# A decoder kernel with a mixture of experts: the experts' rows are gathered by a list of places instead of being scattered into an inbox, and GpSimd makes every second lower comparison of the experts' weights

## The chip, the cores and the metric

One NeuronCore of one Trainium2 chip runs the whole program in one launch. The metric is the device time of one execution in microseconds (us). The engines are named as in the profile: PE (TensorE matmuls), PEld (its weight loads), DVE (VectorE), ACT (ScalarE), POOL (GpSimd) and SP (SyncE, which here only issues DMAs). L12 is line 12 of the kernel before.

## The reference

Six residual layers over x of shape (8, 512, 256), that is 4096 rows of 256 columns: self-attention, cross-attention with quantised weights, a grouped pair of matmuls, a mixture of experts, masked cross-attention, and a quantised pair. The change touches the mixture of experts and the end of the layer ahead of it. Cut to that layer:

```python
def act_quant(x):
    scale = 127.0 / max(max(abs(x)), 1e-5)          # by row
    return clip(round(x * scale), -128, 127) / scale
def weight_quant(w):
    scale = 1.0 / max(mean(abs(w)), 1e-5)           # one number for a matrix
    return clip(round(w * scale), -1, 1) / scale    # -1, 0 or 1
T, E, K, C = 4096, 8, 2, 512                        # C rows of room for each expert
xf = layernorm(x).reshape(T, 256)
probs = softmax(bitlinear(rmsnorm(xf), gate_in_norm_w, gate_w))
topw, topi = top_k(probs, K)
for each expert e:
    pos = cumsum(expert_mask[:, e] > 0) - 1         # place of a row in the expert's room
    tok = the rows with pos < C, in order; empty places give a row of zeros
    h = bitlinear(xf[tok], gp_norm_w[e], gp_w[e])   # gp_w[e]: 1024 x 256
    g, y = split(h)
    out = bitlinear(silu(g) * y, dp_norm_w[e], dp_w[e])   # dp_w[e]: 256 x 512
outputs[tok] += out * topw                          # a row gets what its two experts made
```

Rounding a weight matrix to -1, 0, 1 needs the mean of its magnitudes first (its limits are plus and minus half that mean), and then `(w > half) - (w < -half)`.

## The kernel before

The rows lie in SBUF as `X`, 32 tiles of 128 rows; tile `n` holds rows `128 n` to `128 n + 127`, and a sequence `b` (of B = 8) is four tiles. Each stage is a `Block`: every engine has a program of its own in it, the order of which is written out by hand, semaphores join them, and all engines meet at a barrier between two blocks. The three blocks that matter run one after the other.

**The middle block** (function `middle`) does cross-attention, the grouped pair and the gate. Its loop runs `b` over 12 steps, each sequence in it at several depths at a time. The PSUM banks are handed out in the order of the list `in_order`, round robin over eight; PE takes a bank with `take(bank)` when its last reader has given it free. `gate.u` holds the normalised rows that the experts will get; ACT writes them with `experts_rows(b)`, four instructions for a sequence. The routing is worked out in two parts, sequences 0 to 2 (12 tiles) in the middle block at step b = 7, and sequences 3 to 7 (20 tiles) at the start of the weights block. Each part is `gate.choose` on DVE (softmax, the two best experts; its last instruction gives `kept_made`), `gate.count` on PE (two matmuls that count the rows of each expert, bank "counts"), and `gate.slots` on DVE, which writes `m_slot`: for each row and each of its two experts the place, expert times 512 plus position. At step 7, PE runs `gate.count` ahead of `pair(7, 0)`, and DVE runs `gate.slots` last in the step, behind `add_outputs(6)`, `gate_roots(5)` and `gate_values(6)`.

**Sending.** `gate.send` on POOL scatters every tile of `gate.u` twice (once for each of the two experts of its rows) by an indirect DMA into the DRAM tensor `expert_in` (the inbox, 4096 rows), which SP has filled with zeros early in the middle block by eight DMAs from `f_outT`. 24 sends stand at the end of POOL's middle program, 40 in its weights program.

**The weights block** (first block of `experts`) rounds and transposes the weights of eight experts. Three buffers `g_stage` hold 3072 columns each (2048 of `gp_w`, 1024 of `dp_w`). For expert e: SP loads a buffer once `w_used` says it is free; ACT's `magnitudes(e)` sums the magnitudes; PE's `total(e)` adds them across partitions (one matmul); DVE makes the limits (L2270 to L2273), `g_below` (L2278, two instructions), and `g_w3` (L2284, two instructions, which wait for `w3_used`: PE must have turned the expert before); PE's `turn(e)` transposes `g_w3` in 24 matmuls (L2235, L2241); ACT's `turned_out(e)` copies them to `m_upT` and `m_downT` (L2210). The orders in the loops are

```python
# PE                                  # ACT
for e in range(E):                    for e in range(E):
    turn(e)                               turned_out(e)
    if e + BUFFERS < E:                   if e + BUFFERS < E:
        total(e + BUFFERS)                    magnitudes(e + BUFFERS)
```

SP ends this block by waiting for all 64 sends and loading the rows of experts 0 and 1 from the inbox.

**The experts block** (second block of `experts`) runs the experts one after the other. DVE's `rows(e)` (L2538) waits for `x_loaded`, SP loads expert e + 2 when expert e's rows are used. It lasts from 1504.6 to about 1650 us.

## Time and profile before

| | |
|---|---|
| runs shown (3) | median 2136.21 us, 2127.43 to 2140.68 |
| the profiled execution | 2119.09 us, span 2117.4 us from first to last instruction |
| busy, share of the span | PE 79%, DVE 71%, ACT 68%, POOL 38% |
| middle block | 1079 to 1411 us |
| weights block | 1411 to 1504.6 us |
| experts block | 1504.6 to about 1650 us |

The span is made of blocks between barriers, so the share of busy time says little about any one of them: PE is the busiest engine over the whole and nearly idle in the weights block. The view of the chain that ended last gives nothing here (it stops after one step, at the last line), so the chain within a block is read from the timelines: for each instruction they give its start, its duration, its engine, line, operand names and sizes, how many like it follow (x4), and in square brackets how long its engine stood idle before it and what ended that.

### The profile page before, as it was taken

How to read it: one execution, taken by the hardware profiler on the slowest of the kernel's cores; microseconds unless marked ns; L12 is line 12 of the kernel's file. 1: busy time of each engine (PE TensorE's matmuls, PEld its weight loads, DVE VectorE, ACT ScalarE, POOL GpSimd, SP SyncE). 2: the span in 40 equal slices, each digit the busy share in tenths (PEclk: the TensorE clock that was granted, in tenths of full speed). 3: DMA queues.
4: the chain of work that ended last, by engine and by line, in shares of the span. 5: the costliest groups of instructions: out<-in, count | busy, mean ns of one | idle time of the engine just before them, and what ended most of it. 6: DMA issues, size and time to landing. Idle time of an engine off the chain costs nothing. (4 is left out here: it accounts for less than half of the span.)

```text
span 2117.4 us, 42907 instructions
## 1 busy us (share of the span) xinstructions
PE 1667.2 (79%) x13316; PEld 1070.3 (51%) x13332; DVE 1493.2 (71%) x3066; ACT 1448.9 (68%) x2330; POOL 813.3 (38%) x893
## 2 busy tenths in 40 slices
PE   3889999999999999999758988513365588997677
PEld 1456565555555555555536766412233356665333
DVE  6877777777777877777561566657685487776765
ACT  2888988989898888989704567455387344444745
POOL 0434554545455554545500000048443456563000
PEclk9999999999999999999977989755567789998799
DMA  6222322223222232222151211045211411231002
GB/s 201 54 54 56 69 56 62 61 56 69 56 61 62 56 67 55 56 60 64 34 192 41 80 59 62 1 150 189 90 60 41 130 41 31 29 40 20 1 11 70
DMA packets 173821, 140.00 MB, mean 66 GB/s; under 512 B 83794, under 2 KB 155399, under 8 KB 173366
## 3 DMA queue, kind: packets, MB, share of 16 engines
q1 hardware_dynamic: 166710, 122.78, 21.7%
q0 software_dynamic: 6912, 14.71, 3.5%
q8 instruction: 108, 1.77, 0.4%
q14 instruction: 91, 0.75, 0.1%
HBM read 61.92 MB, written 20.97 MB: 39 GB/s over the span
## 5 line engine op out<-in xcount | busy, mean ns | idle before, releaser
L573 ACT ACTIVATE a_p_hi<-ps,a_probs_up,a_s_scale 128x512 f16<-128x512 f32 x512 | 398.1, 778 | 68.2 <-ACTq L571 66.9
L574 ACT ACTIVATE a_probs<-ps,a_probs_up,a_s_scale 128x512 f32<-128x512 f32 x512 | 398.2, 778 | 0.0
L688 DVE TENSOR_REDUCE a_top<-ps 128x2 f32<-128x1024 f32 x256 | 313.2, 1224 | 119.0 <-DVEq L687 119.0
L920 POOL TENSOR_TENSOR a_p_lo<-a_probs,a_p_hi 128x1024 f16<-128x1024 f32 x128 | 275.9, 2155 | 248.0 <-POOLq L919 205.0
L908 POOL TENSOR_TENSOR a_ops<-a_ident_down,a_top 64x256 f16<-64x256 f32 x256 | 159.8, 624 | 288.5 <-POOLq L903 280.0
L697 DVE TENSOR_TENSOR a_p_lo<-a_probs,a_p_hi 128x1024 f16<-128x1024 f32 x128 | 183.7, 1435 | 39.3 <-DVEq L696 39.3
L453 PE MATMUL ps<-a_v_hi,a_p_hi 128*128 128x65 f16 x2048 | 204.9, 196 | 4.4 <-PEq L448 4.2
L434 PE MATMUL ps<-a_ops 128*128 128x512 f16 x512 | 196.2, 383 | 15.0 <-PEq L432 14.5
L456 PE MATMUL ps<-a_v_lo,a_p_hi 128*128 128x64 f16 x2048 | 204.8, 195 | 0.0
L457 PE MATMUL ps<-a_v_hi,a_p_lo 128*128 128x65 f16 x2048 | 204.7, 196 | 0.0
L453 PEld LDWEIGHTS ps<-a_v_hi,a_p_hi 128*128 128x128 f16 x2048 | 190.9, 99 | 25.7 <-issue 14.9
L420 PE MATMUL ps<-a_qk,a_qd 128*128 128x512 f16 x512 | 152.7, 380 | 59.0 <-PEq L418 57.6
L435 PE MATMUL ps<-a_ops 128*128 128x512 f16 x512 | 196.7, 384 | 0.0
L456 PEld LDWEIGHTS ps<-a_v_lo,a_p_hi 128*128 128x128 f16 x2048 | 190.2, 100 | 12.1 <-issue 1.7
L457 PEld LDWEIGHTS ps<-a_v_hi,a_p_lo 128*128 128x128 f16 x2048 | 190.2, 99 | 0.0
L1189 POOL DMA_INDIRECT expert_in<-gate_u,m_slot x64 | 84.0, 1312 | 118.2 <-POOLq L1185 99.3
L407 PE MATMUL ps<-a_wp,a_oT 128*128 128x256 f32 x512 | 125.9, 390 | 1.1 <-PEq L363 1.1
L670 DVE SCALAR_TENSOR_TENSOR a_qk<-ps,a_qk 128x512 f16<-128x512 f32 x128 | 88.5, 692 | 35.7 <-DVEq L669 35.5
L420 PEld LDWEIGHTS ps<-a_qk,a_qd 128*128 128x128 f16 x512 | 44.3, 97 | 134.9 <-issue 107.1
L378 PE MATMUL ps<-a_xnT,a_wq 128*128 128x512 f16 x384 | 94.7, 383 | 6.3 <-PEq L363 6.2
L407 PEld LDWEIGHTS ps<-a_wp,a_oT 128*128 128x128 f32 x512 | 92.9, 191 | 11.4 <-issue 1.3
L378 PE MATMUL ps<-a_xnT,a_wk 128*128 128x512 f16 x384 | 94.6, 383 | 0.2
(499 smaller groups left out, 3709.4 us busy)
## 6 DMA issues: line engine op xcount, KB each, us to landing
a_ops<-a_qk SPq DMA_DIRECT2D x384, 128.0 KB, 2.3
...
a_qd<-a_qk SPq DMA_DIRECT2D x128, 64.0 KB, 2.2
...
```

The source lines that it names most:

```text
L378: last = nc.tensor.matmul(ps[:, JOB + bank, :], w[:, i, d, c * P:(c + 1) * P], xnT[:, j, d, :], start=(n == d == 0), stop=(n == len(PARTS) ...
L407: last = nc.tensor.matmul(ps[:, JOB + bank, 0:D], oT[:, c, t * P:(t + 1) * P], wp[:, c, :], start=(c % (HC // 2) == 0), stop=(c % (HC // 2 ...
L420: last = nc.tensor.matmul(ps[:, ROW + j % 2, :], qd[:, s, j, :], qk[:, s, K_HI, :], start=True, stop=True)
L434: nc.tensor.matmul(ps[:, st_bank(n), :], ops[:, s, i, A_K, keys], ops[:, s, i, A_Q, :], start=True, stop=False)
L435: nc.tensor.matmul(ps[:, st_bank(n), :], ops[:, s, i, B_K, keys], ops[:, s, i, B_Q, :], start=False, stop=True).then_inc(st_full, 1)
L453: first = nc.tensor.matmul(ps[:, AV, at:at + HD + 1], hi, v_hi[:, k, h, :], start=(k == 0), stop=False)
L456: nc.tensor.matmul(ps[:, AV, at:at + HD], hi, v_lo[:, k, h, :], start=False, stop=False)
L457: last = nc.tensor.matmul(ps[:, AV, at:at + HD + 1], lo, v_hi[:, k, h, :], start=False, stop=(k == KT - 1))
L573: nc.scalar.activation(p_hi[:, h % 2, k, :], scores, ACT.Exp, bias=probs_up[:], scale=s_scale[:])
L574: nc.scalar.activation(probs[:, h % 2, k, :], scores, ACT.Exp, bias=probs_up[:], scale=s_scale[:]).then_inc(st_taken, 1)
L688: nc.vector.tensor_reduce(top[:, c % 2, 2 * pair:2 * pair + 2], ps[:, ROW:ROW + 2, :], AX.X, ALU.max).then_inc(row_taken, 1)
L920: nc.gpsimd.tensor_tensor(p_lo[:, h % 2, 2:KT, :], probs[:, h % 2, 2:KT, :], p_hi[:, h % 2, 2:KT, :], ALU.subtract).then_inc(p_made_pool, 1)
```

## The change

The scatter and its inbox go. In the middle block SP stores the rows themselves, a sequence at a time, into a DRAM tensor `expert_rows` (eight DMAs of 512 KB behind the last weight loads, each waiting for its sequence's `u_made`); the eight DMAs of zeros are gone, and so are POOL's 24 sends there. `gate.slots` moves up on DVE to stand right behind `gate.choose`, `pair(7, 0)` moves ahead of `gate.count` on PE and in the list of banks, and on ACT `f_normalise(7)` moves ahead of `pair_turned(7, 0)` and `experts_rows(4)` from step 7 to step 8.

In the weights block the list of places is turned round: for each of the 4096 places, which row stands in it. DVE makes, for each of the 64 sets of 128 rows, a 0/1 matrix of the place's low part (`low`, 128 columns) and one of its high part (32 columns), the latter also times the tile's number and times the row's number (`numbered`, 64 columns); PE multiplies them, 64 matmuls into one bank; DVE reads the result behind expert 0 into `row_at`. POOL then gathers, four indirect DMAs for an expert, straight to where the experts block reads them (`x_in` is now `gate.u`). Between them POOL makes `below_odd`, the lower comparison of the next odd expert. DVE makes the limits of two experts at a time ahead of the even one, and `total` and `magnitudes` stand one expert later in their loops.

```diff
+            if b < B:
+                in_order += [("pair", b, 0)]
             if b - 1 in CHOICE:
                 in_order += [("counts", CHOICE.index(b - 1))]
-            if b < B:
-                in_order += [("pair", b, 0)]
...
+                for b in range(B):
+                    sp.wait_ge(u_made, b + 1)
+                    sp.dma_start(gate.rows[b * S:(b + 1) * S, :].rearrange("(t p) d -> p t d", p=P),
+                                 gate.u[:, b * TT:(b + 1) * TT, :]).then_inc(gate.stored, 16)
...
+                    if b < B:
+                        pair(b, 0)
                     if b - 1 in CHOICE:
...
                         gate.count(pe, part, bank_of["counts", part])
-                    if b < B:
-                        pair(b, 0)
...
+                    if b == B:
+                        experts_rows(B - 1 - QUANTISE)
...
+                    if b == B - 1:
+                        f_normalise(b)
...
-                    if 0 <= b - QUANTISE < B:
+                    if 0 <= b - QUANTISE < B and b != B - 1:
                         experts_rows(b - QUANTISE)
...
                     if b - 1 in CHOICE:
                         gate.choose(dve, CHOICE.index(b - 1))
+                        bank = bank_of["counts", CHOICE.index(b - 1)]
+                        gate.slots(dve, CHOICE.index(b - 1), bank, free[bank])
...
-                    if b - 1 in CHOICE:
-                        bank = bank_of["counts", CHOICE.index(b - 1)]
-                        gate.slots(dve, CHOICE.index(b - 1), bank, free[bank])
...
-                    sp.wait_ge(gate.sent, 16 * K * NT)
-                    for e in range(2):
-                        load(sp, e, e)
...
+                    pool.wait_ge(row_made, 1)
+                    pool.sem_inc(row_made, -1)
+                    for e in range(E):
+                        for t in range(RT):
+                            nc.gpsimd.indirect_dma_start(
+                                out=x_in[:, e, t, :], out_offset=None, in_=gate.rows,
+                                in_offset=bass.IndirectOffsetOnAxis(ap=row_at[:, e * RT + t:e * RT + t + 1], axis=0),
+                                bounds_check=NT * P - 1, oob_is_err=False).then_inc(x_loaded[e], 16)
+                        if e % 2 == 0:
+                            pool.wait_ge(limits_made, 1)
+                            pool.sem_inc(limits_made, -1)
+                            w = stage[(e + 1) % BUFFERS]
+                            for i, part in ((0, slice(0, W_UP)), (1, slice(W_UP, W_ALL))):
+                                nc.gpsimd.tensor_scalar(below_odd[:, part], w[:, part], minus_half_w[:, 1, i:i + 1], None, ALU.is_lt)
+                            pool.drain().then_inc(below_made, 1)
...
                         turned_out(e)
-                        if e + BUFFERS < E:
-                            magnitudes(e + BUFFERS)
+                        if 1 <= e and e - 1 + BUFFERS < E:
+                            magnitudes(e - 1 + BUFFERS)
...
+                    pe.wait_ge(places_made, 1)
+                    pe.sem_inc(places_made, -1)
+                    for n in range(N):
+                        last = nc.tensor.matmul(ps[:, PLACES, 0:2 * HIGH], low[:, n, :], numbered[:, n, :], start=(n == 0), stop=(n == N - 1))
+                    last.then_inc(places_full, 1)
                     for e in range(E):
                         turn(e)
-                        if e + BUFFERS < E:
-                            total(e + BUFFERS)
+                        if 1 <= e and e - 1 + BUFFERS < E:
+                            total(e - 1 + BUFFERS)
...
+                    nc.vector.tensor_tensor(high, of_places(number[:, 0:HIGH], HIGH), of_rows(high_no, HIGH), ALU.is_equal)
+                    dve.drain()
+                    nc.vector.tensor_tensor(low, of_places(number[:], P), of_rows(low_no, P), ALU.is_equal)
...
+                        nc.vector.tensor_tensor(numbered[:, i * NT:(i + 1) * NT, 0:HIGH], high[:, i * NT:(i + 1) * NT, :],
+                                                number[:, 0:NT].unsqueeze(2).broadcast_to([P, NT, HIGH]), ALU.mult)
+                    nc.vector.tensor_scalar(numbered[:, :, HIGH:2 * HIGH], high, number_p[:], None, ALU.mult)
+                    dve.drain().then_inc(places_made, 1)
...
+                    def rows_at_places():
+                        dve.wait_ge(places_full, 1)
+                        dve.sem_inc(places_full, -1)
+                        nc.vector.tensor_scalar(row_no[:], ps[:, PLACES, 0:HIGH], float(P), None, ALU.mult)
...
+                        nc.vector.tensor_scalar(row_at[:], row_no[:], 0.0, None, ALU.add)
+                        dve.drain().then_inc(row_made, 1)
+
+                    for e in range(E):
+                        j = e % BUFFERS
+                        if e % 2 == 0:
+                            limits(e)
+                            limits(e + 1)
+                            dve.drain().then_inc(limits_made, 1)
...
+                        below_e = below if e % 2 == 0 else below_odd
+                        if e % 2 == 0:
+                            for i, w, part in parts:
+                                nc.vector.tensor_scalar(below[:, part], flat(w), minus_half_w[:, 0, i:i + 1], None, ALU.is_lt)
+                            dve.drain()
+                        else:
+                            dve.wait_ge(below_made, 1)
+                            dve.sem_inc(below_made, -1)
                         if e:
                             dve.wait_ge(w3_used, 1)
                             dve.sem_inc(w3_used, -1)
...
                         dve.drain().then_inc(w_round, 1)
                         dve.drain().then_inc(w_used, 1)
+                        if e == 0:
+                            rows_at_places()
```

**PE, middle block, step 7.** Before: the two counting matmuls of the first part (96 columns) stand between the matmuls of `outputs(6)` (L1483) and those of `pair(7, 0)` (L1459). Names: `f_w2T` is the turned second weight, `outT` the transposed outputs, `c_free0` the bank that is taken.

```order
L1483 MATMUL ps<-f_xnT,f_wT 128x512
L1143 MATMUL ps<-gate_kept,gate_upto 128x96 [waits gate_kept_made,c_free0]
L1144 MATMUL ps<-gate_kept,gate_all 128x96
L1459 MATMUL ps<-f_w,f_w2T 128x257 [waits c_w2T_out,c_b1_set,c_free1]
L1459 MATMUL ps<-f_w,f_w2T 128x257 x7
L1496 MATMUL ps<-ident,f_outT 128x128 [waits c_outT_out,c_free2]
L1496 MATMUL ps<-ident,f_outT 128x128 x3
```

Now (the same rows of the changed program):

```order
L1472 MATMUL ps<-f_xnT,f_wT 128x512
L1448 MATMUL ps<-f_w,f_w2T 128x257 [waits c_w2T_out,c_b1_set,c_free0]
L1448 MATMUL ps<-f_w,f_w2T 128x257 x7
L1144 MATMUL ps<-gate_kept,gate_upto 128x96 [waits gate_kept_made,c_free1]
L1145 MATMUL ps<-gate_kept,gate_all 128x96
L1485 MATMUL ps<-ident,f_outT 128x128 [waits c_outT_out,c_free2]
L1485 MATMUL ps<-ident,f_outT 128x128 x3
```

The 8 matmuls of `pair(7, 0)` stand ahead of the wait for `gate_kept_made` now, and the counts use the bank behind the pair's.

**PE, weights block, from the first `turn` on.** `g_w_sum` is what `magnitudes` made (the matmul is `total`), `g_w` with `ident` are the transposes of `turn`. Before:

```order
L2225 MATMUL ps<-g_w_sum,g_ones 128x2 [waits g_w_part] x3
L2235 MATMUL ps<-ident,g_w 128x128 [waits g_w_round]
L2235 MATMUL ps<-ident,g_w 128x128 x15
L2241 MATMUL ps<-ident,g_w 128x128 x8
L2225 MATMUL ps<-g_w_sum,g_ones 128x2 [waits g_w_part]
L2235 MATMUL ps<-ident,g_w 128x128 [waits g_w_round,g_w_out]
L2235 MATMUL ps<-ident,g_w 128x128 x15
L2241 MATMUL ps<-ident,g_w 128x128 x8
L2225 MATMUL ps<-g_w_sum,g_ones 128x2 [waits g_w_part]
```

Now:

```order
L2244 MATMUL ps<-g_w_sum,g_ones 128x2 [waits g_w_part] x3
L2272 MATMUL ps<-gate_u 128x64 [waits g_places_made]
L2272 MATMUL ps<-gate_u 128x64 x63
L2254 MATMUL ps<-ident,g_w 128x128 [waits g_w_round]
L2254 MATMUL ps<-ident,g_w 128x128 x15
L2260 MATMUL ps<-ident,g_w 128x128 x8
L2254 MATMUL ps<-ident,g_w 128x128 [waits g_w_round,g_w_out]
L2254 MATMUL ps<-ident,g_w 128x128 x15
L2260 MATMUL ps<-ident,g_w 128x128 x8
L2244 MATMUL ps<-g_w_sum,g_ones 128x2 [waits g_w_part]
L2254 MATMUL ps<-ident,g_w 128x128 [waits g_w_round,g_w_out]
L2254 MATMUL ps<-ident,g_w 128x128 x15
```

The 64 matmuls on the matrices of places (they lie in `gate_u`) stand ahead of `turn(0)`; `turn(1)` follows `turn(0)` at once, and `total(3)` follows `turn(1)`.

**DVE, weights block, experts 2 and 3.** L2270 and L2315 read the sum of magnitudes. Before (expert 2, and the first row of 3):

```order
L2270 TENSOR_SCALAR m_w_mean<-ps 128x1 [waits g_w_total]
L2270 TENSOR_SCALAR m_w_mean<-ps 128x1
L2272 TENSOR_SCALAR g_half_w<-m_w_mean 128x2
L2273 TENSOR_SCALAR g_minus_half_w<-m_w_mean 128x2
L2278 TENSOR_SCALAR g_below<-g_stage,g_minus_half_w 128x2048
L2278 TENSOR_SCALAR g_below<-g_stage,g_minus_half_w 128x1024
L2284 SCALAR_TENSOR_TENSOR g_w<-g_stage,g_half_w,g_below 128x2048 [waits g_w3_used]
L2284 SCALAR_TENSOR_TENSOR g_w<-g_stage,g_half_w,g_below 128x1024
L2270 TENSOR_SCALAR m_w_mean<-ps 128x1 [waits g_w_total]
```

Now (from the last two rows of the limits of expert 2 to the rounding of expert 3):

```order
L2317 TENSOR_SCALAR g_half_w<-m_w_mean 128x2
L2318 TENSOR_SCALAR g_minus_half_w<-m_w_mean 128x2
L2315 TENSOR_SCALAR m_w_mean<-ps 128x1 [waits g_w_total]
L2315 TENSOR_SCALAR m_w_mean<-ps 128x1
L2317 TENSOR_SCALAR g_half_w<-m_w_mean 128x2
L2318 TENSOR_SCALAR g_minus_half_w<-m_w_mean 128x2
L2342 TENSOR_SCALAR g_below<-g_stage,g_minus_half_w 128x2048
L2342 TENSOR_SCALAR g_below<-g_stage,g_minus_half_w 128x1024
L2351 SCALAR_TENSOR_TENSOR g_w<-g_stage,g_half_w,g_below 128x2048 [waits g_w3_used]
L2351 SCALAR_TENSOR_TENSOR g_w<-g_stage,g_half_w,g_below 128x1024
L2351 SCALAR_TENSOR_TENSOR g_w<-g_stage,g_half_w,g_below_odd 128x2048 [waits g_below_made,g_w3_used]
L2351 SCALAR_TENSOR_TENSOR g_w<-g_stage,g_half_w,g_below_odd 128x1024
```

Each `g_w_total` is a wait for one more expert's sum. Two of them stand ahead of expert 2's comparison now; expert 3 has no comparison of its own on DVE but a wait for `g_below_made`, which POOL gives.

## Rows read from the trace of the kernel before

**Rows 1.** Busy time by stretch: us, then PE, PEld, DVE, ACT, POOL busy (instructions), clock, DMA share, GB/s.

```profile
1428.00:1495.00 67.00, 21.70 (x180) 19.98 (x180) 48.16 (x64) 37.71 (x45) 55.40 (x37) 0.53 0.45 150
```

**Rows 2.** Groups of DVE's instructions in the weights block, 1428 to 1495 us.

```profile
L2284 DVE SCALAR_TENSOR_TENSOR g_w<-g_stage,g_half_w,g_below 128x2048 bf16<-128x2048 f32 x8 | 18.8, 2351 | 14.8 <-DVEq L2282 9.8 <-PEq L2243 4.9
L2278 DVE TENSOR_SCALAR g_below<-g_stage,g_minus_half_w 128x2048 bf16<-128x2048 f32 x8 | 10.3, 1286 | 0.7
L2284 DVE SCALAR_TENSOR_TENSOR g_w<-g_stage,g_half_w,g_below 128x1024 bf16<-128x1024 f32 x8 | 10.2, 1279 | 0.0
L2278 DVE TENSOR_SCALAR g_below<-g_stage,g_minus_half_w 128x1024 bf16<-128x1024 f32 x8 | 6.0, 748 | 0.0
```

**Rows 3.** Timeline of DVE in the weights block: first limits, three of the eight roundings.

```profile
1428.31 0.22 DVE L2270 TENSOR_SCALAR m_w_mean<-ps 128x1 f32<-128x1 f32 x2 [0.63 <-DVEq L2267]
...
1431.00 3.55 DVE L2284 SCALAR_TENSOR_TENSOR g_w<-g_stage,g_half_w,g_below 128x2048 bf16<-128x2048 f32 x2
...
1437.70 3.55 DVE L2284 SCALAR_TENSOR_TENSOR g_w<-g_stage,g_half_w,g_below 128x2048 bf16<-128x2048 f32 x2 [0.18 <-DVEq L2282]
...
1491.35 3.55 DVE L2284 SCALAR_TENSOR_TENSOR g_w<-g_stage,g_half_w,g_below 128x2048 bf16<-128x2048 f32 x2 [0.36 <-DVEq L2282]
```

**Rows 4.** Timeline of ACT in the weights block: copies out and magnitudes.

```profile
1437.68 1.03 ACT L2210 ACTIVATE m_downT<-ps 128x1024 bf16<-128x1024 bf16 x1
...
1450.08 1.92 ACT L2201 ACTIVATE g_junk<-g_stage 128x2048 bf16<-128x2048 f32 x1
...
1453.12 0.19 ACT L2201 ACTIVATION_READ_ACCUMULATOR g_junk<-g_stage 128x1 f32 x1
...
1498.18 1.03 ACT L2210 ACTIVATE m_downT<-ps 128x1024 bf16<-128x1024 bf16 x1
```

**Rows 5.** Timeline of PE in the weights block: `total(4)` and the start of `turn(2)`.

```profile
1453.51 0.56 PE L2225 MATMUL ps<-g_w_sum,g_ones 128*128 128x2 f32 x2 [4.58 <-PEq L2224]
1453.93 1.87 PE L2235 MATMUL ps<-ident,g_w 128*128 128x128 bf16 x16
```

**Rows 6.** Timeline of POOL in the weights block: one send that waited, the last send.

```profile
1438.00 2.90 POOL L1189 DMA_INDIRECT expert_in<-gate_u,m_slot  x1 [0.30 <-issue]
...
1498.68 0.97 POOL L1189 DMA_INDIRECT expert_in<-gate_u,m_slot  x1 [0.31 <-issue]
```

**Rows 7.** The instructions on `e_r` on POOL: ns min/median/max.

```profile
L2358 POOL TENSOR_SCALAR e_r<-e_a,e_per_row x32: 478/479/1552, 1508.6 to 1601.7; 128x256 f16<-128x256 f32 x32
```

**Rows 8.** Two groups of POOL's instructions over the whole span.

```profile
L920 POOL TENSOR_TENSOR a_p_lo<-a_probs,a_p_hi 128x1024 f16<-128x1024 f32 x128 | 275.9, 2155 | 248.0 <-POOLq L919 205.0 <-POOLq L926 26.6 <-POOLq L885 11.6
...
L940 POOL TENSOR_SCALAR a_lny_tmp<-a_lny_tmp 128x4 f32<-128x4 f32 x21 | 4.6, 221 | 3.6 <-issue 3.6
```

**Rows 9.** Timeline of DVE and of POOL in the masked attention: the same operation beside POOL and alone.

```profile
1694.90 2.52 DVE L2107 SCALAR_TENSOR_TENSOR X<-b_got,m_share,X 128x256 f32<-128x256 f32 x2
1695.16 1.97 POOL L2712 TENSOR_TENSOR x_s<-x_s,x_top 128x1024 f32<-128x1024 f32 x1 [1.58 <-POOLq L2711]
...
1708.94 1.66 DVE L2107 SCALAR_TENSOR_TENSOR X<-b_got,m_share,X 128x256 f32<-128x256 f32 x4
```

**Rows 10.** Timeline of the end of the middle block, PE, DVE and ACT.

```profile
1347.24 0.24 PE L1143 MATMUL ps<-gate_kept,gate_upto 128*128 128x96 bf16 x1 [6.78 <-PEq L1379]
1354.34 1.29 DVE L1969 TENSOR_TENSOR X<-ps,X 128x512 f32<-128x512 f32 x2 [7.40 <-DVEq L1967]
1369.91 0.71 DVE L1155 TENSOR_TENSOR_SCAN gate_before<-gate_ones_col,ps 128x12 f32<-128x12 f32 x8
1374.93 0.17 DVE L1892 TENSOR_SCALAR gate_square<-mean_var 128x4 f32<-128x4 f32 x1 [0.17 <-issue]
1382.44 1.29 DVE L1969 TENSOR_TENSOR X<-ps,X 128x512 f32<-128x512 f32 x2 [0.49 <-DVEq L1967]
1405.22 2.07 ACT L1732 ACTIVATE gate_u<-X,gate_u_shift,gate_u_factor 128x256 f32<-128x256 f32 x4
```

**Rows 11.** Timeline of SP and DVE between the weights block and the experts block.

```profile
1500.77 0.92 SPq L2144 DMA_DIRECT2D e_x_in<-expert_in  x2
...
1504.79 1.23 DVE L2538 TENSOR_TENSOR e_a<-e_x_in,e_up_n 128x1024 f32<-128x1024 f32 x1
```

116 lines of the change are left out of this document (59 added, 57 removed).

## The prediction

> **What bounds the kernel now.** The blocks run one after the other, so I read the change's two blocks by their own timelines: first the busy times by stretch, then the groups of DVE, then the timelines of DVE, ACT, PE and POOL of the weights block, then the end of the middle block.
>
> In the weights block DVE is busy 48.2 of 67 us, POOL 55.4, ACT 37.7, PE 21.7 [rows 1]. No engine is full; a ring of waits sets the pace. DVE's first limits start at 1428.31 and its last rounding ends at 1491.35 + 3.55 = 1494.90 [rows 3]: 66.6 us for eight experts, 16.65 for a pair. The shortest step is seen between the first two roundings: the first ends at 1434.55, PE turns, the next starts at 1437.70, 3.15 later [rows 3]. So a rounding can end every 3.55 + 3.15 = 6.7 us. What the eight steps take beyond that is in the 14.8 us that DVE stood idle ahead of L2284 [rows 2]: PE holds `turn(1)` back behind `total(3)`, and so on. **The comparison L2278 (1286 + 748 ns [rows 2]) lies inside the 3.15 us in which PE turns**, so it costs next to nothing on the path. POOL's sends end at 1499.65 [rows 6], also after DVE; SP then loads rows at 1500.77 and the next block starts at 1504.79 [rows 11].
>
> **Places, first expert (added, on the path).** DVE must make the matrices of places ahead of its first limits. Two-input operations: 2351 ns for 2048 columns and 1279 for 1024 [rows 2], so 1.05 ns a column and 0.2 fixed. `high` has 2048 columns: 2.35; `low` 8192: 8.8; the tile's number, two of 1024: 2.55; the row's number, one input, 2048: 1.3 as L2278. The small casts and subtractions and their drains I take at 1.5, and the two added slot copies at 0.2. Sum 16.7 us; nothing covers it, since POOL and PE wait for it. The limits of experts 0 and 1 then start at 1445.0. The limits of one take 2.69 - 2.03 = 0.66 [rows 2, 3]; two, then the comparison, then the rounding: 1445.0 + 1.3 + 0.1 + 2.05 + 3.55 = 1452.0. Meanwhile PE makes 64 matmuls on two-byte numbers; 16 transposes take 1.87, 0.117 each [rows 5], so 7.5 us, to about 1452, hidden by the rounding. DVE reads the result (three small operations): 1453.2. POOL now issues four gathers ahead of its first comparison, although the limits have long been there: 0.97 + 0.30 each [rows 6], 5.5 us with the wake-up, to 1458.7.
>
> **POOL's comparison.** No row shows one. Nearest is a one-input `TENSOR_SCALAR` of 256 columns, 479 ns, beside 221 for 4 columns [rows 7, 8]: 1.02 ns a column. Two instructions, 3072 columns: 3.1 + 0.4 = 3.55 us. The upper end is the two-input rate, 2155 ns for 1024 columns [rows 8], 6.5 us. I take 3.55, as the form is the same. By the Trainium skill (GPSIMD Engine Reference, 3.1) a loop that makes a truth value takes 2.03 cycles an element unless it is unrolled, an estimate of 5.2 us, and the sum would be some 7 us worse. DVE waits for it: rounding 1 starts at 1458.7 + 3.55 + 0.3 and ends at **1466.3, against 1441.25 before**.
>
> **The pair's ring (added, on the path).** For experts 2 and 3 DVE makes both limits first, so expert 2 waits for `total(3)`, which stands behind `turn(1)`; and `magnitudes(3)` stands behind `turned_out(1)`. From the end R of an odd rounding: copies end at R + 4.15 (1434.55 to 1438.71 [rows 3, 4]); magnitudes 3.25 (1450.08 to 1453.31) and 0.2 until PE starts [rows 4, 5]; the sum 0.56 [rows 5]; limits 0.66 and drains 0.3: R + 9.1. Comparison 2.05, rounding 3.55, then 6.7 for the odd one, since PE must turn the even: R + 21.4. From the second pair on, PE does `total(4)` between `turn(2)` and `turn(3)`, which comes when `magnitudes(4)` ends, 1.2 us after the odd rounding: R + 22.6. Loads (issued when a rounding ends) land before ACT wants them; in each pair they have over 10 us.
>
> **The port between DVE and POOL.** Beside POOL's L2712 (1695.16 to 1697.13) two DVE operations take 2.52 us, where four take 1.66 [rows 9]: the second began when POOL ended. The other way, a send of 0.97 lasts 2.90 inside a rounding [rows 6]. So I add the whole 3.55 us to each of the three later pairs, in which POOL's comparison is due at the same time as DVE's. The Trainium skill (SBUF — State Buffer, Who interferes with whom) speaks against this change with the same rule: whichever of the two starts first has the shared port for its whole instruction and the other stands still; by it the trace agrees, and without it the sum is 10.6 us less. POOL's eight gathers between two comparisons take 10.2 us, some 14 with such stalls, and fit into the 26 of a pair.
>
> Last rounding: 1466.3 + (21.4 + 3.55) + 2 x (22.6 + 3.55) = 1543.5, against 1494.9: **+48.6 us**. At the end of the block the wait for the sends and SP's loads go: ACT ends 1499.21 - 1494.90 = 4.3 after the last rounding [rows 3, 4], plus 3.3 for the barrier (2.9 from the end of SP's issue at 1501.69 to the next block [rows 11], some 4 at the end of the middle [rows 10]), 7.6, against 9.7 before: -2.1. The experts block is unchanged: DVE found its rows at once before [rows 11], so loading them early buys nothing there.
>
> **The middle block (a gain).** PE stood idle 6.78 us ahead of the counts, DVE 7.40 us ahead of the add at 1354.34, and then DVE had `slots` (1369.91 to 1374.93, 5.0 us) on the path to the add at 1382.44, where it waited only 0.49 [rows 10]. Now PE's pair fills the wait for the choice, and `slots` falls into DVE's idle time. Behind it DVE's next steps start 1.4 us earlier, need no wait for ACT's squares (1.4), and have no `slots` in between (5.0): 7.8 to 8.3 at the add. ACT's chain to the last row of `gate.u` (1405.22 + 2.07 [rows 10]) follows and loses an `experts_rows` besides (2.1, part of it idle time). I take -9; at least -4 (only `slots`, less 1 for new waits), at most -14 (both idle times in full). The zeros were behind the loads that matter and no engine waited for them: 0. SP's stores run beside other work; the last waits for ACT's last row, where POOL's last send stood before: 0.
>
> **Sum.** +48.6 - 2.1 - 9 = +37.5 us. On the profiled execution that is 2119.1 + 37.5 = 2156.6; it lies 17 us under the median of the runs, so against the median I forecast 2136.2 + 37 = **2173 us**.
>
> **Rivals.**
> *A. The port does not serialise* (DVE's comparison and rounding run beside POOL's): 10.6 us less, 2163. For it: the two engines also overlap without loss where DVE reads one input. Against: [rows 9]. 0.20.
> *B. The pair's ring does not bind* (faster than before): if the sum of magnitudes for the next odd expert were there in time, a pair would take 2 x 6.7 = 13.4; the last rounding ends at 1466.3 + 40.2 = 1506.5, +11.6 - 2.1 - 9 = 0.5, and with the middle at -14 it is -4.5: 2132 to 2137. It decides where a pair takes under 13.2 us. For it: DVE's 14.8 us of idle time, which moving `total` is to win back. Against: three waits in a row that each stand in the written order. 0.09, and 0.02 of it faster by over 1%, if the middle gives more than I see.
> *C. POOL's comparison goes at the slow rate*: 2.95 more in each of four pairs, 12 us, 2185. 0.15.
> *D. The middle gives back nothing*, because another wait takes over at the end (ACT's quantising chain): +46, 2182. 0.05.
> The forecast as worked out: 0.51.
>
> **Range.** Low end: A with a middle of -14, 2158, less 5 for the spread of the runs (2127 to 2141), 2153. High end: C with a middle of -4, 2190. That leaves out B and a little above, under 2 in 10. A measurement of this kernel can tell about 1%, 21 us. Slower by over that (above 2157.6): the forecast, C, D, and A but for its lower part, 0.85. Within 1%: B and that part, 0.12. Faster: 0.03.
>
> **What would show it.** In the changed kernel's timeline: DVE's matrices take 16 to 17 us from the end of `slots`; it idles some 10 us ahead of its second rounding; 9 us or more lie between the end of an odd rounding and the next even comparison, that idle time ended by the wait for the sum of magnitudes; the last rounding ends about 132 us after the block's start, where it ended 83 after it (1411.7 to 1494.9); L2342's two instructions last longer than 1286 and 748 ns where POOL compares; PE's 6.78 us wait in the middle is gone and the middle is some 9 us shorter. I am wrong if the limits of the odd expert are there when the even one wants them, or if POOL's comparison ends well before DVE's even rounding at no cost to it.

## The result

The changed kernel takes 2170.5 us (median of four runs, 2164.2 to 2176.8) against 2131.8 for the kernel before: a ratio of 1.0168, interval 1.0133 to 1.0203, or 28 to 43 us more. The forecast was 2173 in a range of 2153 to 2190, and slower.

The two profiled executions lie further apart than the medians, 2119.1 and 2176.8 us, since that of before lies below every timed run of it and that of the changed kernel is its slowest. So I compare block by block. The busy times of the kernel before in three stretches (up to the weights block, the weights block, the rest); the columns are the stretch and its length, PE, PEld, DVE, ACT and POOL busy (instructions), the granted clock, DMA share, GB/s:

```profile
0.00:1411.70 1411.70, 1196.40 (x10828) 765.55 (x10828) 1005.61 (x1996) 1073.06 (x1767) 537.54 (x557) 0.94 0.27 68
1411.70:1504.60 92.90, 25.85 (x210) 23.60 (x210) 60.95 (x163) 48.16 (x57) 59.13 (x40) 0.52 0.51 168
1504.60:2117.40 612.80, 444.96 (x2278) 281.10 (x2294) 426.65 (x908) 327.67 (x506) 216.59 (x296) 0.84 0.20 47
```

The same three of the changed kernel:

```profile
0.00:1408.49 1408.49, 1200.16 (x10828) 769.18 (x10828) 1005.81 (x1999) 1071.80 (x1767) 513.44 (x534) 0.93 0.26 65
1408.49:1556.56 148.07, 29.93 (x274) 27.28 (x274) 85.57 (x169) 48.13 (x57) 76.73 (x42) 0.53 0.36 124
1556.56:2174.90 618.34, 448.34 (x2294) 282.61 (x2294) 422.03 (x908) 326.12 (x506) 216.81 (x296) 0.84 0.17 41
```

The whole loss is in the weights block: 148.1 us against 92.9, **+55.2**. The rest shows +5.5, but four variants of the kernel before in which nothing of that stretch was touched took 617.6 to 620.7 us there (below): the 612.8 is part of what made that execution fast, not what the change cost.

DVE's timeline in the weights block of the changed kernel (start, duration, instruction, idle time ahead of it and what ended it):

```profile
1425.99 2.28 DVE L2301 TENSOR_TENSOR gate_u<-g_number,g_high_no 128x2048 bf16<-128x2048 f32 x1
1428.35 8.69 DVE L2303 TENSOR_TENSOR gate_u<-g_number,g_low_no 128x8192 bf16<-128x8192 f32 x1
...
1440.20 0.23 DVE L2315 TENSOR_SCALAR m_w_mean<-ps 128x1 f32<-128x1 f32 x2 [0.23 <-DVEq L2312]
...
1443.67 3.55 DVE L2351 SCALAR_TENSOR_TENSOR g_w<-g_stage,g_half_w,g_below 128x2048 bf16<-128x2048 f32 x2
...
1463.45 3.55 DVE L2351 SCALAR_TENSOR_TENSOR g_w<-g_stage,g_half_w,g_below_odd 128x2048 bf16<-128x2048 f32 x2 [15.18 <-DVEq L2349]
1467.32 0.23 DVE L2315 TENSOR_SCALAR m_w_mean<-ps 128x1 f32<-128x1 f32 x2 [0.32 <-DVEq L2312]
...
1475.33 0.22 DVE L2315 TENSOR_SCALAR m_w_mean<-ps 128x1 f32<-128x1 f32 x2 [7.28 <-issue]
...
1476.08 7.13 DVE L2342 TENSOR_SCALAR g_below<-g_stage,g_minus_half_w 128x2048 bf16<-128x2048 f32 x2 [0.17 <-issue]
1483.40 4.12 DVE L2351 SCALAR_TENSOR_TENSOR g_w<-g_stage,g_half_w,g_below 128x2048 bf16<-128x2048 f32 x2 [0.19 <-DVEq L2349]
1490.77 3.55 DVE L2351 SCALAR_TENSOR_TENSOR g_w<-g_stage,g_half_w,g_below_odd 128x2048 bf16<-128x2048 f32 x2 [3.24 <-DVEq L2349]
...
1548.18 3.55 DVE L2351 SCALAR_TENSOR_TENSOR g_w<-g_stage,g_half_w,g_below_odd 128x2048 bf16<-128x2048 f32 x2 [3.24 <-issue]
1556.56 0.06 DVE L2646 MEMSET e_above<- 128x1 f32 x1 [4.83 <-PEq L2174]
```

Read it against [rows 3]. The matrices come first; the limits start 31.7 us into the block (16.6 before). The second rounding stands 15.18 us. Then a pair repeats three times: 7.2 to 7.7 us for the odd expert's sum, a comparison of 7.13 us that took 1.95 before, a rounding, 3.24 us of PE's turning, a rounding. The last ends at 1551.73, 143.2 us into the block (83.2 before).

POOL's timeline beside it, the last gather ahead of the first comparison, and the first two comparisons:

```profile
1453.46 1.00 POOL L2198 DMA_INDIRECT gate_u<-expert_rows,g_row_at  x1 [0.30 <-issue]
1454.50 8.28 POOL L2207 TENSOR_SCALAR g_below_odd<-g_stage,g_minus_half_w 128x2048 bf16<-128x2048 f32 x2
1464.00 2.77 POOL L2198 DMA_INDIRECT gate_u<-expert_rows,g_row_at  x1 [1.21 <-issue]
...
1476.20 9.72 POOL L2207 TENSOR_SCALAR g_below_odd<-g_stage,g_minus_half_w 128x2048 bf16<-128x2048 f32 x2 [0.26 <-issue]
```

And the groups of both comparisons, 1425 to 1560 us, by shape:

```profile
L2207 POOL TENSOR_SCALAR g_below_odd<-g_stage,g_minus_half_w 128x2048 bf16<-128x2048 f32 x4 | 24.9, 6217 | 11.6 <-POOLq L2204 11.3 <-issue 0.3
L2342 DVE TENSOR_SCALAR g_below<-g_stage,g_minus_half_w 128x1024 bf16<-128x1024 f32 x4 | 18.5, 4636 | 0.0
L2207 POOL TENSOR_SCALAR g_below_odd<-g_stage,g_minus_half_w 128x1024 bf16<-128x1024 f32 x4 | 12.6, 3148 | 0.0
```

In the three pairs in which the engines meet, DVE's second instruction (1024 columns, 748 ns [rows 2]) lasts 5935 ns: it starts at 1477.4, stands until POOL's first ends, 6.47 us after 1476.20, and then runs. DVE's rounding behind it is not held in this way. Its first instruction, by shape from 1475 to 1488 us:

```profile
L2351 DVE SCALAR_TENSOR_TENSOR g_w<-g_stage,g_half_w,g_below 128x2048 bf16<-128x2048 f32 x1 | 2.9, 2928 | 0.2 <-DVEq L2349 0.2
```

It starts at 1483.40, 2.5 us before POOL's second instruction ends at 1485.92, and takes 0.58 us more than its 2351 ns [rows 2].

The ring on ACT and PE in the second pair, the magnitudes of expert 3 and the sum:

```profile
1471.19 1.92 ACT L2220 ACTIVATE g_junk<-g_stage 128x2048 bf16<-128x2048 f32 x1
```

```profile
1440.15 3.57 PE L2272 MATMUL ps<-gate_u 128*128 128x64 bf16 x64 [11.37 <-PEq L2270]
...
1474.62 0.56 PE L2244 MATMUL ps<-g_w_sum,g_ones 128*128 128x2 f32 x2 [4.58 <-ACTq L2222]
```

The magnitudes start 4.2 us after the odd rounding's end (1467.00), the sum at 7.6, DVE's limits at 8.3.

### The profile page after: what moved, and what is told of

Its sections match the earlier page's. It is cut to its first block and busy times, and to the rows that moved or that the text cites. A ratio compares the mean times of both kernels' runs of the same rounds, so it can differ in the third digit from the quotient of the medians.

```text
span 2174.9 us, 43002 instructions
## 1 busy us (share of the span) xinstructions
PE 1678.4 (77%) x13396; PEld 1079.1 (50%) x13396; DVE 1513.4 (70%) x3075; ACT 1446.1 (66%) x2330; POOL 807.0 (37%) x871
## 5 line engine op out<-in xcount | busy, mean ns | idle before, releaser
L434 PE MATMUL ps<-a_ops 128*128 128x512 f16 x512 | 195.9, 383 | 14.8 <-PEq L432 14.4
L420 PE MATMUL ps<-a_qk,a_qd 128*128 128x512 f16 x512 | 153.2, 381 | 60.2 <-PEq L418 58.9
L407 PEld LDWEIGHTS ps<-a_wp,a_oT 128*128 128x128 f32 x512 | 93.1, 191 | 11.4 <-issue 1.3
L386 PE MATMUL ps<-a_wv,a_xnT 128*128 128x512 f16 x384 | 93.4, 379 | 0.2
```

The lines of the kernel that those rows point to most:

```text
L407: last = nc.tensor.matmul(ps[:, JOB + bank, 0:D], oT[:, c, t * P:(t + 1) * P], wp[:, c, :], start=(c % (HC // 2) == 0), stop=(c % (HC // 2 ...
L420: last = nc.tensor.matmul(ps[:, ROW + j % 2, :], qd[:, s, j, :], qk[:, s, K_HI, :], start=True, stop=True)
L434: nc.tensor.matmul(ps[:, st_bank(n), :], ops[:, s, i, A_K, keys], ops[:, s, i, A_Q, :], start=True, stop=False)
```

## The experiments

Times are ratios to the kernel before of the same chip, whose medians there are 2131.9 us (dve_below, pairs_dve, pool_third, pool_first), 2130.0 (pool_pieces, middle_only, totals_only, middle_totals), 2137.2 (middle_late_sends, rows_early, four_buffers) and 2136.0 (four_late_two): compare the ratios, not the medians. The three kernels with POOL's comparison have 4 runs each, the others 9 to 12. "Block" is the length of the weights block in the profiled execution, "rest" what follows it; the kernel before has 92.9 and 612.8 us, the changed one 148.1 and 618.3.

| kernel | median us | ratio (interval) | block | rest |
|---|---|---|---|---|
| dve_below | 2121.7 | 0.9952 (0.9925 to 0.9979) | 103.0 | 618.8 |
| pairs_dve | 2138.8 | 1.0039 (1.0016 to 1.0063) | 117.9 | 617.5 |
| pool_third | 2147.4 | 1.0078 (1.0047 to 1.0110) | 127.9 | 619.3 |
| pool_first | 2163.3 | 1.0145 (1.0104 to 1.0187) | 142.8 | 620.1 |
| pool_pieces | 2173.1 | 1.0202 (1.0169 to 1.0236) | 152.1 | 617.7 |
| middle_only | 2129.7 | 0.9986 (0.9966 to 1.0006) | 92.4 | 617.6 |
| totals_only | 2133.1 | 1.0008 (0.9988 to 1.0028) | 94.3 | 619.6 |
| middle_totals | 2127.5 | 0.9978 (0.9959 to 0.9998) | 93.2 | 619.0 |
| middle_late_sends | 2125.5 | 0.9944 (0.9919 to 0.9968) | 93.9 | 620.7 |
| rows_early | 2124.3 | 0.9933 (0.9914 to 0.9952) | 101.7 | 617.1 |
| four_buffers | 2122.1 | 0.9926 (0.9901 to 0.9951) | 96.3 | 625.7 |
| four_late_two | 2119.1 | 0.9926 (0.9901 to 0.9951) | 98.5 | 620.8 |

### Which part costs: dve_below and pairs_dve

dve_below takes POOL's comparison and the pairing out of the changed kernel:

```diff
-                        if e % 2 == 0:
-                            limits(e)
-                            limits(e + 1)
-                            dve.drain().then_inc(limits_made, 1)
+                        limits(e)
...
-                        if e % 2 == 0:
-                            for i, w, part in parts:
-                                nc.vector.tensor_scalar(below[:, part], flat(w), minus_half_w[:, 0, i:i + 1], None, ALU.is_lt)
-                            dve.drain()
-                        else:
-                            dve.wait_ge(below_made, 1)
-                            dve.sem_inc(below_made, -1)
+                        for i, w, part in parts:
+                            nc.vector.tensor_scalar(below_e[:, part], flat(w), minus_half_w[:, e % 2, i:i + 1], None, ALU.is_lt)
+                        dve.drain()
```

> The changed kernel with every lower comparison back on DVE (1.95 us each) and each expert's limits made when its turn comes; the list of places, the gathers and the later totals stay. Theory G (the 57 us come from GpSimd's share: its comparison of 8.3 to 9.7 us, DVE held beside it, and limits made in pairs): first rounding ends at 1447.2 as in the changed kernel, then an expert costs DVE 6.7 us (0.7 limits, 1.95, 3.55, 0.5 between), 7 x 6.7 = 47, last rounding at about 1494 against 1551.7, so about 2114 us, 1 % under the kernel before. Rival P (the list of places, its gathers and the stores are what costs): still above 2150 us.

pairs_dve is the same, but `limits(e)` and `limits(e + 1)` stay together ahead of the even expert:

> The changed kernel with every lower comparison on DVE but the limits still made for two experts at a time. Separates the order of the limits from GpSimd's work. Theory G with the ring of the pair: from the second pair on DVE waits some 8.3 us for the odd expert's total of magnitudes, then does 2 x (1.95 + 3.55) and gaps: 20.6 to 21 us a pair against 28.2; last rounding at about 1515, 36 us before the changed kernel: 2134 us, so the pairing alone costs some 20 us over one at a time. Rival (only GpSimd's comparison and the port cost, the order of limits is harmless): about 2114 us as with limits one at a time.

dve_below came out at 0.9952, faster than the kernel before, so rival P falls: the list of places and its gathers cost some 10 us in the block, and the rest of the change gives back more. The block goes 148.1, 117.9, 103.0: **POOL's comparison is worth 30.2 us of the 55.2, making the limits in pairs 14.9, and everything else in the block 10.1**, taken out in this order. By the ratios the first two are 28 and 19 us of 2132. The pairing is no harmless side of the edit. DVE in pairs_dve, the odd expert's limits and its rounding in the second pair:

```profile
1457.64 0.22 DVE L2308 TENSOR_SCALAR m_w_mean<-ps 128x1 f32<-128x1 f32 x2 [7.80 <-issue]
...
1467.20 3.55 DVE L2339 SCALAR_TENSOR_TENSOR g_w<-g_stage,g_half_w,g_below_odd 128x2048 bf16<-128x2048 f32 x2 [1.08 <-DVEq L2337]
```

The same 7 to 8 us as in the changed kernel stand here without any work on POOL. A later pair takes 22.5 us (28.2 changed); I had expected 21 and left out this 1.08 of PE's turning and the 1.55 us by which even limits wait too.

dve_below missed its number by nearly 8 us. Its last roundings, the last gather and the next block (DVE, then POOL):

```profile
1451.58 0.22 DVE L2308 TENSOR_SCALAR m_w_mean<-ps 128x1 f32<-128x1 f32 x2 [1.55 <-issue]
...
1486.29 3.54 DVE L2337 SCALAR_TENSOR_TENSOR g_w<-g_stage,g_half_w,g_below_odd 128x2048 bf16<-128x2048 f32 x2 [0.19 <-DVEq L2335]
1500.74 0.06 DVE L2632 MEMSET e_above<- 128x1 f32 x1 [10.91 <-PEq L2174]
```

```profile
1496.35 1.00 POOL L2198 DMA_INDIRECT gate_u<-expert_rows,g_row_at  x1 [0.30 <-issue]
```

An expert costs 7.7 us there, not 6.7, for the limits wait 1.2 to 2.1 us each; and the gathers end 7.5 us after DVE and set the block's end.

### What POOL's comparison costs: pool_third, pool_first, pool_pieces

pool_third leaves POOL only the columns of `w_down`; DVE compares the other 2048 of the odd expert:

```diff
-                            for i, part in ((0, slice(0, W_UP)), (1, slice(W_UP, W_ALL))):
+                            for i, part in ((1, slice(W_UP, W_ALL)),):
...
+                        for i, w, part in (parts if e % 2 == 0 else parts[:1]):
+                            nc.vector.tensor_scalar(below_e[:, part], flat(w), minus_half_w[:, e % 2, i:i + 1], None, ALU.is_lt)
```

> The changed kernel with GpSimd comparing only the 1024 columns of w_down of every second expert; DVE compares their 2048 columns of w_up itself (1.29 us). If GpSimd's 8.3 to 9.7 us go by columns: 2.8 to 3.3 us, DVE held 2 to 3 us in place of 5.2, first pair 5.8 us shorter, later pairs 22.6 in place of 28.2: 22.7 us less, 2148 us. Rival (what counts is the ring of limits alone): no more than 6 us less, 2164 us.

0.0078 above before, 2147.4 us, and a block of 127.9, 20 less. POOL's instruction in it, ns min/median/max:

```profile
L2207 POOL TENSOR_SCALAR g_below_odd<-g_stage,g_minus_half_w x4: 2876/3880/3883, 1443.8 to 1507.4; 128x1024 bf16<-128x1024 f32 x4
```

2.88 us alone, 3.88 beside DVE, whose comparison now takes 2.81 in place of 7.13. The cost goes by POOL's columns.

pool_first moves the comparison ahead of its expert's gathers and of the wait for the list:

```diff
                     for e in range(E):
+                        (POOL's comparison of expert e + 1, if e is even)
+                        if e == 0:
+                            pool.wait_ge(row_made, 1)
+                            pool.sem_inc(row_made, -1)
...
                         for t in range(RT):
                             nc.gpsimd.indirect_dma_start(
```

> The changed kernel with GpSimd's comparison put ahead of the gathers of its expert, so the first one does not stand behind four gathers and behind the list. By my sum: it runs beside DVE's first comparison, which becomes some 5.2 us longer, but the second rounding then starts at about 1455.6 in place of 1463.5: 7.8 us less, 2162 us; later pairs the same. Rival: the first comparison is as dear wherever it stands (DVE held for the whole of it): no change, 2170 us.

2163.3 us, block 5.3 shorter. DVE's first comparison and second rounding (7.15 and 1451.40), and POOL's first comparison:

```profile
1436.85 7.15 DVE L2343 TENSOR_SCALAR g_below<-g_stage,g_minus_half_w 128x2048 bf16<-128x2048 f32 x2 [0.17 <-issue]
...
1451.40 3.55 DVE L2352 SCALAR_TENSOR_TENSOR g_w<-g_stage,g_half_w,g_below_odd 128x2048 bf16<-128x2048 f32 x2 [2.04 <-DVEq L2350]
```

```profile
1436.96 9.73 POOL L2200 TENSOR_SCALAR g_below_odd<-g_stage,g_minus_half_w 128x2048 bf16<-128x2048 f32 x2 [33.03 <-POOLq L2197]
```

The second rounding starts 47.7 us into the block, 55.0 in the changed kernel: the 7.3 us of queueing were real. The last rounding ends 7.8 us sooner, and 2.5 of that are lost at the end, where the idle time ahead of the next block is 7.36 us in place of 4.83: the last gather ends at 1543.99, behind DVE (1539.10) and ACT (1543.41).

pool_pieces cuts an expert's comparison into 12 instructions of 256 columns:

```diff
-                            for i, part in ((0, slice(0, W_UP)), (1, slice(W_UP, W_ALL))):
+                            for i, part in [(int(s >= W_UP), slice(s, s + 256)) for s in range(0, W_ALL, 256)]:
```

> The changed kernel with GpSimd's comparison of an expert cut into 12 instructions of 256 columns in place of two of 2048 and 1024. If DVE is held until GpSimd's instruction ends, DVE's comparison beside it takes 2 to 3 us in place of 7.1, a later pair 4 us less, 2158 us. If it is held for as long as GpSimd has work (or GpSimd's pieces cost much each), 2170 us or above: 12 pieces at some 0.1 us more each are 1.2 us a pair.

The groups of its pieces and of DVE's second instruction:

```profile
L2207 POOL TENSOR_SCALAR g_below_odd<-g_stage,g_minus_half_w 128x256 bf16<-128x256 f32 x48 | 54.7, 1155 | 0.8 <-issue 0.5 <-POOLq L2204 0.3
...
L2342 DVE TENSOR_SCALAR g_below<-g_stage,g_minus_half_w 128x1024 bf16<-128x1024 f32 x4 | 3.6, 911 | 0.0
```

The hold lasts one instruction: DVE's 5935 ns fell to 911 on average. Yet the block grew by 4 us, to 152.1: the 12 pieces take 10.8 us with DVE idle (8.28 for the two instructions) and 14.8 in place of 9.7 beside DVE, where now POOL waits for DVE (the first three pieces take 2252 ns each, 913 alone), and the odd rounding waits 9.8 us for them. So the mechanism was the one I gave 2158 us for, and the time the other's: what was saved at the port went into POOL's own time.

### The other two parts, alone: middle_only, totals_only, middle_totals, middle_late_sends

middle_only puts the middle block's new order (of PE, ACT and DVE) into the kernel before; totals_only only moves magnitudes and totals one expert later; middle_totals does both. Of totals_only (PE's `total` moves in the same way):

```diff
-                        if e + BUFFERS < E:
-                            magnitudes(e + BUFFERS)
+                        if 1 <= e and e - 1 + BUFFERS < E:
+                            magnitudes(e - 1 + BUFFERS)
...
```

> The kernel before with the middle block's new order alone (PE's pair ahead of the counts, slots right behind the choice, f_normalise of the last sequence and the experts' rows earlier). My step was -9 us (-4 to -14): 2123 us. Rival (the granted clock of the middle block takes it back, as the 9.3 us that the changed kernel's profiled execution was late at 1337): within 3 us of the kernel before, 2129 to 2134 us.

> The kernel before with the magnitudes and the total of an expert one step later in ACT's and PE's order, and nothing else. DVE idled 14.8 us between its first and last rounding, for the total and for w3; if that order is its cause, an expert costs 6.7 us in place of 7.7: 7 us less to 14 less, 2117 to 2125 us. Rival (the loads of the weights or PE's turning set the pace): 2131 us.

> The kernel before with both orders, the middle block's and the later totals, without the list of places, the gathers and GpSimd's comparison. If the two add up: 16 to 23 us less than the kernel before, 2108 to 2115 us, the fastest of all. If they do not: as the better of the two alone.

None of the forecast gains came: 0.9986, 1.0008 and 0.9978; middle_totals is 0 to 9 us under the kernel before, where 16 to 23 were expected. totals_only did take DVE's idle time away (the later limits wait 1.2 to 1.8 us, w3 no more), and its last rounding ends 75.7 us into the block, not 83.2. But the block is 94.3 long. The last rounding and the next block's start on DVE, and the last send on POOL:

```profile
1504.37 3.55 DVE L2284 SCALAR_TENSOR_TENSOR g_w<-g_stage,g_half_w,g_below 128x2048 bf16<-128x2048 f32 x2 [0.19 <-DVEq L2282]
1526.58 0.06 DVE L2589 MEMSET e_above<- 128x1 f32 x1 [18.66 <-PEq L2168]
```

```profile
1520.67 0.97 POOL L1189 DMA_INDIRECT expert_in<-gate_u,m_slot  x1 [0.30 <-issue]
```

**In the kernel before POOL's 40 sends set the end of the block**: they end at 1499.65 [rows 6], 4.75 us after DVE's last rounding, and DVE's 14.8 us of idle time [rows 2] were covered by them.

For the middle, where sequences 3, 6 and 7 of `gate.u` start on ACT (us), by kernel. "To the add" runs from sequence 3's start to DVE's second add of the outputs (1382.44 in the kernel before [rows 10]), which the new order was to bring forward:

| kernel | order | sends | seq. 3 | seq. 6 | seq. 7 | next block | to the add | 3 to 6 |
|---|---|---|---|---|---|---|---|---|
| before | old | 1375.9 to 1407.8 | 1328.06 | 1397.06 | 1405.22 | 1411.70 | 54.4 | 69.0 |
| totals_only | old | 1383.9 to 1414.6 | 1336.02 | 1419.17 | 1427.32 | 1432.25 | 54.4 | 83.2 |
| middle_only | new | 1349.7 to 1381.3 | 1323.76 | 1397.09 | 1405.24 | 1410.16 | 60.2 | 73.3 |
| middle_totals | new | 1348.4 to 1379.1 | 1322.25 | 1400.22 | 1408.37 | 1413.29 | 63.4 | 78.0 |
| middle_late_sends | new | 1372.7 to 1404.0 | 1323.32 | 1382.76 | 1399.99 | 1409.26 | 46.3 | 59.4 |
| changed | new | none | 1337.33 | 1397.08 | 1405.24 | 1408.49 | 46.7 | 59.8 |

totals_only has the middle block of the kernel before, word for word, and yet takes 14 us longer from sequence 3 to 6. Up to the add the two agree; the difference lies among the sends, where ACT stood twice ahead of its copy of `gate_rT`:

```profile
1399.66 1.02 ACT L1761 ACTIVATE gate_rT<-ps 128x1024 bf16<-128x1024 bf16 x1 [6.81 <-ACTq L1760]
1418.03 1.02 ACT L1761 ACTIVATE gate_rT<-ps 128x1024 bf16<-128x1024 bf16 x1 [8.19 <-ACTq L1760]
```

In middle_only the slots are ready 24.6 us after sequence 3's start (46.7 before), so POOL sends sooner, into the chain that the order was to shorten. middle_late_sends keeps the new order and holds the sends back:

```diff
-                pool.wait_ge(u_made, gate.SEQUENCES[0])
+                pool.wait_ge(u_made, 6)
```

> The kernel before with the middle block's new order, but GpSimd's first 24 sends held back until six sequences' rows are made. In middle_only they ran from 1349.7 to 1380.9 and the stretch from ACT's row normalising of sequence 3 to that of sequence 7 took 81.5 us; in the kernel before 77.2, in the changed kernel and its five variants, without sends, 67 to 68. If the sends beside it took the gain of the order: that stretch falls to 68 to 71 us, though the block still waits for the last send, so the time is only 0 to 5 us under the kernel before, 2125 to 2130. If the gain needs something else of the changed kernel: 77 us or more.

Sequences 3 to 6 fall to 59.4 us, as in the changed kernel; then the sends, now beside the last sequence, cost 9 us there (17.2 from 6 to 7, against 8.2 in the others), so that sequences 3 to 7 take 76.7, not the 68 to 71 expected. DVE's second add in this kernel and in the changed one, then PE and ACT in the place of the 9 us:

```profile
1369.66 1.29 DVE L1974 TENSOR_TENSOR X<-ps,X 128x512 f32<-128x512 f32 x2 [0.23 <-DVEq L1972]
```

```profile
1383.98 1.29 DVE L1963 TENSOR_TENSOR X<-ps,X 128x512 f32<-128x512 f32 x2 [0.23 <-DVEq L1961]
```

```profile
1400.20 0.35 PE L1518 MATMUL ps<-gate_gwT,gate_rT 128*128 128x8 bf16 x8 [10.56 <-issue]
```

```profile
1398.85 1.02 ACT L1761 ACTIVATE gate_rT<-ps 128x1024 bf16<-128x1024 bf16 x1 [10.54 <-ACTq L1760]
```

So the new order is worth 7.7 to 8.1 us at the add (54.4 to 46.3 and 46.7) where no send runs beside it; in the kernel before sends run beside the last 6.5 us of these 54.4, in which DVE waits 0.5. Behind the add the kernel before has sends and the changed one has none, and no run takes that apart: a kernel with the old order and without sends was not tried. The time of middle_late_sends, 0.9944, is lower than this one execution's middle explains (the next block starts about when it does in middle_only), and I leave that open.

### A version that beats both: rows_early, four_buffers, four_late_two

rows_early starts from dve_below and reads the list of places ahead of the first rounding:

```diff
+                        if e == 0:
+                            rows_at_places()
                         for i, w, part in parts:
                             nc.vector.scalar_tensor_tensor(out=w3[:, part], in0=flat(w), scalar=half_w[:, e % 2, i:i + 1], in1=below_e[:, part],
                                                            op0=ALU.is_gt, op1=ALU.subtract)
                         dve.drain().then_inc(w_round, 1)
                         dve.drain().then_inc(w_used, 1)
-                        if e == 0:
-                            rows_at_places()
```

> The kernel with all comparisons on DVE (dve_below), and the list's last step, from which GpSimd's gathers start, made ahead of DVE's first rounding in place of behind it. In dve_below the last rounding ended at 1489.8, ACT at 1494.1, and the 32 gathers at 1497.4, 3.4 us before the next block. If the gathers set the block's end, they start and end 3.8 us earlier and the block is 3.2 us shorter (then ACT's end binds): 2118 us. If they do not: 2121.7 us, unchanged.

The first gather starts 2.9 us sooner (37.1 into the block, 40.0 in dve_below), the last ends 1.2 sooner, the block is 1.3 shorter (3.8 and 3.2 were expected); 0.9933 against 0.9952 is no difference that these intervals can tell.

four_buffers adds a fourth weight buffer (the sum of the list goes to the bank of the counts) and moves the last 6 gathers to the next block:

```diff
-            BUFFERS = 3
+            BUFFERS = 4
...
-                    for e in range(E):
-                        for t in range(RT):
+                    gathers(0, LATE)
...
+                    gathers(LATE, E * RT)
                     round_rows(0)
```

> As rows_early, with four weight buffers in place of three, the magnitudes of expert e + 3 behind the turning of expert e, and the last 6 of the 32 gathers in the next block. If the ring of dve_below (limits of expert e + 2 wait for the magnitudes behind the turning of expert e, 1.2 to 2.1 us of DVE's idle time an expert) is what kept an expert at 7.7 us in place of 6.7: last rounding 6 to 7 us earlier, block 93 us from 103, 10 us less than dve_below: 2112 us, 1 % under the kernel before. Rival (the loads of the weights or the gathers, lengthened by DVE's comparisons, set the pace): 2118 us.

> As four_buffers, but only the last 2 of the 32 gathers stand in the next block. In four_buffers the weights block took 96.3 us (rows_early 101.7), but what follows it 625.7 us against 617.1: GpSimd's rounding of the first rows stood behind six gathers, 1494.8 to 1503.9, where DVE had the rows ready some 4 us after the block's start. If that is the price: two gathers (2.6 us) fit ahead of that moment, the rest is back at 617 to 620 us, and the block ends 3.4 us after the 30th gather, some 97.5 us: 2115 us, 7 us under four_buffers. If the rest stays at 625 us, the cause is another: 2122 us.

The block fell to 96.3 us, but the rest rose to 625.7. DVE's fifth rounding and the next block's start, and the last of POOL's late gathers in four_buffers:

```profile
1463.37 3.55 DVE L2343 SCALAR_TENSOR_TENSOR g_w<-g_stage,g_half_w,g_below 128x2048 bf16<-128x2048 f32 x2 [1.60 <-PEq L2259]
...
1494.17 0.06 DVE L2637 MEMSET e_above<- 128x1 f32 x1 [4.83 <-PEq L2183]
```

```profile
1502.92 1.00 POOL L2141 DMA_INDIRECT gate_u<-expert_rows,m_row_at  x1 [0.30 <-issue]
```

The limits no longer wait; DVE's rounding waits for PE's turning instead, 1.2 to 1.6 us: 7.4 us an expert (7.7 in dve_below), a third of what I hoped for. With two late gathers (four_late_two: `LATE = 30`) the rest is back at 620.8 and the block is 98.5, near what was expected (617 to 620, 97.5). The medians are 2122.1 and 2119.1, but on two chips, and the ratios are equal: the 7 us that I expected between them are not there. Both are 0.5 to 1.0% under the kernel before, the lowest ratios of the study, though the intervals do not set them apart from rows_early, dve_below and middle_late_sends.

## Why the prediction was right

The direction, the place and the mechanism held. The sum came as near as it did by luck: one term was 11.4 us too small, two others gave back 6.3 more than forecast, and the medians lie 4 us closer than the blocks add up to. The first three rows are parts of the fourth; the pairs took 53.65 us before.

| term of the sum | predicted us | in the profiled executions |
|---|---|---|
| matrices of places, ahead of the first limits | +16.7 | +15.1 |
| end of rounding 1 | +25.05 | +29.0 |
| three later pairs | 77.25 | 84.7 |
| last rounding | +48.6 | +60.0 |
| end of the block | -2.1 | -4.9 |
| middle (from sequence 3's rows on) | -9 | -12.5 |
| sum | +37.5 | +42.7; medians +38.7 |

The spans of the profiled executions differ by 57.5 us: these 42.7, the 9.3 by which sequence 3 starts later, and the 5.5 of the rest.

**Places: right.** 8.69 us for 8192 columns where 8.8 stood. The two operations on two-byte numbers took 2.35 and 0.75 us, for 2.55 and 1.3. PE's 64 matmuls took 3.57 us, not 7.5, and were hidden as said.

**POOL's comparison: the mis-sized term.** I took 3.55 us, from a rate of 1.02 ns a column, with 6.5 as the upper end. It takes 8.28 alone and 9.72 beside DVE: outside my bounds. By 5.45 us for 2048 columns (8.28 less the 2.83 of the other instruction) it is 2.7 ns a column. The row I went by wrote f16 from one multiply and add; that a comparison has the same form did not mean the same rate (whether the comparison or the type makes the difference was not tried). The first pair shows it in full: 4.7 more on POOL, less what the shorter list gave back, 3.9 on rounding 1. So rival C happened in kind: its own price was 12 us, and the last rounding came 11.4 later than forecast. The Trainium skill (GPSIMD Engine Reference, Performance pitfalls for Q7 kernels, not 3.1 as I had it) gives a loop that makes a truth value 2.03 cycles an element, from which I had the estimate of 5.2 us; its direction was right, the measured 8.28 is 1.6 times that.

**The port: right in kind, priced by the wrong length.** I added the whole of POOL's comparison, 3.55 us, to each later pair. The measured hold is 5.2 us on DVE's comparison (7.13 for 1.95) and 0.6 on its rounding (4.12 for 3.55), less than POOL's 9.72. The hold ended with POOL's first instruction; the second ran beside DVE's rounding and PE's turning. The row I went by [rows 9] had a DVE operation with two inputs held by POOL; here the one with one input was held and the one with two hardly. That is why 6 us too little on POOL became 2.3 to 2.8 us too little in a pair. Rival A falls, and with it what I had put down for it, that the engines overlap without loss where DVE reads one input: the comparison reads one and stood 5.2 us. The Trainium skill (SBUF — State Buffer, Who interferes with whom) says that the one that comes first has the shared pair for its whole instruction; for the comparison the trace agrees, with 5935 ns for 748, and pool_pieces shows the "instruction" in it; for the rounding it does not, which lost 0.58 us where POOL had 2.5 us to go.

**The pair's ring: right.** R + 9.1 was the forecast for the odd limits; in the second pair DVE's comparison, right behind them, starts at 1476.08 - 1467.00 = 9.08, in the later two, which I put at 10.3, 10.2 and 10.7. Rival B falls: pairs_dve prices the ring alone at 15 us.

**Gathers ahead of the comparison: right.** POOL starts comparing 46.0 us into the block (47.0 predicted); pool_first moved the second rounding by 7.3 us and won back 5.3.

**End of the block: sized too small.** 4.8 us from last rounding to next block, for 7.6. I had added a barrier of 3.3 to ACT's end, where it took 0.5. What I had not seen is what the sends hid in the kernel before; it changes nothing here, where the last gather ends at 1551.41, 0.3 us ahead of DVE's last rounding, and ACT's copies only at 1556.05, but all in the versions that beat it.

**The middle: right in the order, and one term missed.** The forecast was 7.8 to 8.3 us at the second add; it came 7.7 sooner (rival D falls). PE's wait ahead of the counts is not gone but 3.3 us in place of 6.8. From the add to the next block the changed kernel takes 24.5 us, the kernel before 29.3; 3.2 of these 4.8 us lie behind sequence 7's rows, where the last send and its barrier stood, and the forecast had put that place at 0. What I missed is what the sends do to the other engines: the same stretch of the same middle took 41.8 us in totals_only, and with sends in its midst the order's gain turns round (60.2 and 63.4 us to the add). In the profiled execution itself the gain does not show, because the block's earlier part was 9.3 us late: sequence 3 starts at 1337.33 against 1328.06, with the granted clock from 1200 to 1260 us at 0.74 against 0.91. The start of sequence 3 ranges from 1325.9 to 1337.3 over nine kernels with the stores and from 1322.3 to 1336.0 over five with the inbox; whether the stores add a few us there stays open.
